# Carrying x, a 65-wide state and a 32-wide memory through the end of a four-layer scan network instead of the 512-wide rows

## What is computed

```
# four layers, 64 wide: norm, silu, complex exponential filter along the sequence,
# residual; norm, 64-256-64 network with silu, residual
h   = layers(LN(x) @ Win.T + bin)
x1  = x + LN(norm(h) @ Wout.T + bout)          # 512 wide
xn  = LN(x1)
q   = xn @ Wq.T                                # 64 wide
top = the 8 best of 128 slots by (q Wr.T)(keys Wr.T).T / sqrt(48) + log_rel
w   = softmax over these 8 of q keys.T / 8 + log_rel
mem = (w @ values) @ Wvd.T @ Wvu.T             # 512 -> 32 -> 512
g   = gate(var(xn), gelu(xn @ Wu1.T + bu1) @ Wu2.T + bu2)   # one number per row
out = x1 + LN(xn + g * mem)
```

## Time and profile before

| | us |
|---|---|
| median of three runs | 251.32 |
| the profiled execution's own time | 250.35 |
| its span in the trace | 248.5 |
| busy in the span: TensorE, VectorE, ScalarE, GpSimd | 196.7, 181.2, 128.3, 89.4 |

### The profile page before, as it was taken

How to read it: one execution, slowest core, us unless ns; L and a number is a source line. 1 busy time by engine, 2 the same in 40 slices (tenths; PEclk the granted TensorE clock), 3 DMA queues, 4 the chain that set the end, 5 groups by cost and what they waited for, 6 DMA issues and landing times.

```text
span 248.5 us, 3501 instructions
## 1 busy us (share of the span) xinstructions
PE 196.7 (79%) x1148; PEld 145.2 (58%) x1148; DVE 181.2 (73%) x507; ACT 128.3 (52%) x306; POOL 89.4 (36%) x118
## 2 busy tenths in 40 slices
PE   2699596389959998878888759999999999399600
PEld 2699495377848787767776525565556555143200
DVE  7799895557784777767663174977797775889993
ACT  4328728246543667575565644343243329587640
POOL 8213333433342443533334332121212110048772
PEclk9999989799997999999999999999999999979965
DMA  5999900000000000000000000000000000003346
GB/s 197 425 415 419 258 9 4 0 0 1 3 0 0 3 0 0 4 0 0 3 0 3 0 0 1 1 3 0 0 0 0 0 3 1 0 0 120 135 169 253
DMA packets 5407, 15.09 MB, mean 61 GB/s; under 512 B 909, under 2 KB 1773, under 8 KB 4366
## 3 DMA queue, kind: packets, MB, share of 16 engines
q1 hardware_dynamic: 5390, 14.88, 16.2%
HBM read 10.68 MB, written 4.19 MB: 60 GB/s over the span
## 4 chain that ended last, share of the span: by engine, by line
PE 49%; DVE 25%; POOL 10%; ACT 9%; issue 4%; POOLq 0%; DVEq 0%; ACTq 0%
PE bank L1164 15%; PE bank L1110 12%; POOL RS L328 8%; PE bank L1140 5%; PE bank L1057 4%; DVE Z L735 3%; DVE SS L729 3%; PE bank L1207 3%; PE bank L1070 2%; ACT SQ L449 2%; PE bank L1151 2%; DVE XT L966 2%; DVE X L972 2%; PE bank L1038 2%; PE bank L1095 1%
## 5 line engine op out<-in xcount | busy, mean ns | idle before, releaser
L328 POOL TENSOR_TENSOR RS<-SS,nhalf 128x4 f32<-128x4 f32 x36 | 43.1, 1209 | 72.0 <-DVE SS L729 71.8
L1164 PE MATMUL bank<-SW_,Y 128*128 128x384 f32 x128 | 43.9, 485 | 0.0
L729 DVE TENSOR_REDUCE SS<-SQ 128x4 f32<-128x260 f32 x36 | 15.1, 423 | 26.1 <-ACT SQ L449 25.0
L1164 PEld LDWEIGHTS bank<-SW_,Y 128*128 128x128 f32 x128 | 23.9, 190 | 17.0 <-issue 4.2
L1110 PE MATMUL bank<-ffst,HD 128*128 128x128 f32 x256 | 33.5, 287 | 0.0
L1110 PEld LDWEIGHTS bank<-ffst,HD 128*128 128x128 f32 x256 | 32.4, 205 | 0.3
L449 ACT ACTIVATE SQ<-bank 128x256 f32<-128x256 f32 x36 | 13.8, 383 | 29.4 <-PE bank L1110 18.1
L476 ACT ACTIVATE HD<-bank,b1r 128x512 f32<-128x512 f32 x32 | 20.3, 684 | 12.1 <-PE bank L1095 12.1
L1057 PE MATMUL bank<-ident,Z 128*128 128x128 f32 x64 | 11.5, 306 | 18.0 <-DVE Z L735 17.9
L1057 PEld LDWEIGHTS bank<-ident,Z 128*128 128x128 f32 x64 | 7.3, 151 | 23.7 <-DVE Z L735 23.7
L809 DVE SCALAR_TENSOR_TENSOR X<-bank,OR,X 128x512 f32<-128x512 f32 x16 | 11.3, 746 | 12.3 <-POOL OR L346 12.2
(11 more groups left out here) (219 smaller groups left out, 376.1 us busy)
## 6 DMA issues: line engine op xcount, KB each, us to landing
XT<-in_xT SPq DMA_DIRECT2D x4, 1024.0 KB, 11.4
X<-in_x SPq DMA_DIRECT2D x4, 1024.0 KB, 14.1
out<-X SPq DMA_DIRECT2D x8, 512.0 KB, 2.8
w1r<-in_w1d SPq DMA_DIRECT2D x1, 516.0 KB, 11.6
lt<-in_late SPq DMA_DIRECT2D x1, 385.5 KB, 19.3
w2r<-in_w2n SPq DMA_DIRECT2D x1, 256.0 KB, 7.1
...
```

The costliest lines, as they stand in the source:

```text
L328: pool.tensor_tensor(RS[:, g, :], SS[:, g, :], nhalf[:, :], ALU.pow).then_inc(done, 1)
L729: dve.tensor_reduce(SS[:, g, :], SQ[:, g, :, :], AX.X, ALU.add).then_inc(done, 1)
L1164: last = pe.matmul(SBK[t % 4][:, 0:SW], XNT[:, t % 4, c * P:(c + 1) * P], SW_[:, c, :], start=False, stop=(c == VC - 1))
```

## The change

The end no longer makes the 512-wide rows before it needs them. The weights of the memory's queries, of the gate and of the memory's way back are stacked beside the folded output matrix (65 columns: 64 and the bias) into M, 289 columns, centred by its column means (`column_sums`, `centre_m`). x times M is taken per tile (`project_x`, four matmuls of 289 columns into the one bank LB, and a copy, `x_out`): tiles 0 to 4 in steps 1 to 3, tiles 5 to 15 in steps 16 to 19. Norms of the 512-wide rows come out of Gram products in 65 dimensions (`gram`, `cross`, `first_variance`). `mixed` and `project` add the state's part to x's part; scores are matmuls over 64 dimensions. The memory product is 64 columns wide (`memory`), its norm comes from `dots` (32 wide), GpSimd works out the factors of a batch of tiles, VectorE writes them into the 128-wide F, which is transposed and multiplied by FM (512 columns), and `finish` adds x. All 20 steps stand before the end; `keep_busy` is gone, first_h(3) stands in step 0, and GpSimd does no 512-wide product. The score rows are 256 wide instead of 384. There are five late stages instead of six.

```diff
+ZD = DIM + 1
+MA, MQ, MU = ZD + UH + BOT, ZD + UH, ZD
+MW = ZD + UH + BOT + VB
+AW = MW - ZD
+SW = 2 * NSLOT
...
-        EARLY = 2
-        LATE0, LATES = 4, 6
-        POOL_TILES = (1, 4, 7, 10)
-        LAG = 2
+        LATE0, LATES = 4, 5
+        LATE_OUTS = (2, 4, 5, 7, 8)
+        XSTEP = {1: (0, 1), 2: (2, 3), 3: (4,), 16: (5,), 17: (6, 7, 8),
+                 18: (9, 10, 11), 19: (12, 13, 14, 15)}
+        SELS = PAIRS
+        BATCHES = ((0, 4), (4, 8), (8, 12), (12, 14), (14, 16))
+        LAST = [e // 2 - 1 for _, e in BATCHES]
+        MIXLAG = 3
+        FIN = {4: (0,), 5: (1,), 6: (2,), 7: (3,), 8: (4,), 9: (5, 6), 10: (7,)}
...
                 if g == 0:
+                    sp.dma_start(c6[:, :], c64).then_inc(s_c64, 16)
+                    sp.dma_start(WOR[:, :], woutb).then_inc(s_m, 16)
                     sp.dma_start(w2r[:, :], w2n).then_inc(s_w2, 16)
+                    sp.dma_start(M[:, :, ZD:MW], mraw).then_inc(s_m, 16)
                 if g == 1:
...
+                if s == 0:
+                    centre_m(2)
+                    centre_m(3)
...
+            centre_m(0)
+            centre_m(1)
+            for s in range(STEPS):
...
+            for a, b in BATCHES:
+                gs, w, zr, rr, al, fo, yg = (GX[:, i, a:b] for i in range(7))
+                pool.wait_ge(dots_done, b // 2)
+                pool.wait_ge(es_inv, b // 2)
+                link(pool.tensor_tensor(gs, RES[:, a:b], GA[:, 4, a:b], ALU.mult))
+                link(pool.tensor_tensor(w, gs, XQ[:, a:b, 1], ALU.mult))
+                link(pool.tensor_tensor(w, w, XQ[:, a:b, 0], ALU.add))
+                link(pool.tensor_tensor(w, w, gs, ALU.mult))
+                link(pool.tensor_tensor(w, w, K2P[:, a:b], ALU.add))
+                link(pool.tensor_tensor(zr, w, nhalf[:, 0:b - a], ALU.pow))
+                pool.tensor_tensor(yg, zr, gs, ALU.mult)
+                link(pool.tensor_tensor(rr, zr, R16[:, a:b], ALU.mult))
+                pool.tensor_tensor(F[:, a:b, ZD], rr, NXM[:, a:b], ALU.mult)
+                link(pool.tensor_scalar(al, rr, 1.0, 1.0, ALU.mult, ALU.add))
+                pool.tensor_tensor(fo, al, RHO[:, a:b], ALU.mult).then_inc(mix_ready, 1)
...
+            def mix_rows():
+                act.wait_ge(bp_mm, 1)
+                act.activation(M[:, :, 0:ZD], LB[:, 0:VC * ZD].rearrange("p (c d) -> p c d", c=VC),
+                               ACT.Copy).then_inc(bp_read, 1)
+            def column_means():
+                act.wait_ge(cs_mm, 1)
+                act.activation(CSUM[:, :], LB[:, 0:MW], ACT.Copy, scale=-1.0 / VOCAB).then_inc(cs_read, 1)
+            def x_out(t):
+                act.wait_ge(xa_mm, t + 1)
+                act.activation(XA[:, t, :], LB[:, 0:MW], ACT.Copy).then_inc(xa_read, 1)
...
+                for t in XSTEP.get(s, ()):
+                    x_out(t)
...
+            for s in range(STEPS):
+                if s == 0:
+                    mix_rows()
+                    column_means()
+                step(s)
+                if s == 0:
+                    ffn_out()
+            for p in range(PAIRS):
+                scaled(2 * p)
+                scaled(2 * p + 1)
+                gelu(p)
+                if p >= 1:
+                    qt_out(p - 1)
+            qt_out(PAIRS - 1)
+            act.wait_ge(ln_in, 1)
+            act.activation(GA[:, 3, :], GA[:, 2, :], ACT.Ln).then_inc(ln_out, 1)
+            for k in range(SELS + MIXLAG):
+                if k < SELS:
+                    exps(k)
                     e_out(k)
...
+                    y_out(k)
+                if k == 1:
+                    act.wait_ge(sig_in, 1)
+                    act.activation(GA[:, 9, :], GA[:, 8, :], ACT.Exp, scale=-1.0).then_inc(sig_out, 1)
+                if k == 2:
+                    act.wait_ge(gate_in, 1)
+                    act.activation(GA[:, 16, :], GA[:, 15, :], ACT.Exp, scale=-1.0).then_inc(gate_out, 1)
+                for p in FIN.get(k, ()):
+                    f_out(p)
...
+            def project(p):
+                for t in (2 * p, 2 * p + 1):
+                    dve.wait_ge(am_mm, 2 * p + 2)
+                    dve.wait_ge(rho_done, t // GT + 1)
+                    dve.scalar_tensor_tensor(out=T[:, t, 0:AW], in0=AB[t // GT][:, t % 2, 0:AW], scalar=RHO[:, t:t + 1],
+                                             in1=XA[:, t, ZD:MW], op0=ALU.mult, op1=ALU.add).then_inc(t_done, 1)
...
+            first_variance(2)
+            gram(3)
+            unscore(0)
+            project(2)
+            unscore(1)
+            project(3)
+            unscore(2)
+            project(4)
+            unscore(3)
+            first_variance(3)
+            project(5)
+            unscore(4)
+            gate_variance()
+            project(6)
+            unscore(5)
+            project(7)
+            unscore(6)
+            unscore(7)
+            for k in range(SELS + MIXLAG):
+                if k < SELS:
+                    select(k)
+                for i in range(len(BATCHES)):
+                    if LAST[i] + MIXLAG == k:
+                        factors(i)
+                if k == 0:
+                    for p in range(5):
+                        learned(p)
+                if k == 1:
+                    for p in range(5, PAIRS):
+                        learned(p)
+                    gate_learned()
                     gate_sum()
...
+                if k == 2:
                     gate_mean()
...
+                    gate_level()
+                if 0 <= k - 1 < SELS:
+                    dots(k - 1)
+                if k == 2:
+                    gate()
+                for p in FIN.get(k, ()):
+                    finish(2 * p)
+                    finish(2 * p + 1)
...
+            def project_x(t, s):
+                pe.wait_ge(m_done, VC)
+                pe.wait_ge(cs_read, 1)
+                if t >= 1:
+                    pe.wait_ge(xa_read, t)
+                if s > LATE0:
+                    pe.wait_ge(late_read, LATE_OUTS[LATES - 1])
+                g, j = t // GT, t % GT
+                for c in range(VC):
+                    last = pe.matmul(LB[:, 0:MW], XT[:, g, c, j * P:(j + 1) * P], M[:, c, :], start=(c == 0),
+                                     stop=(c == VC - 1))
+                last.then_inc(xa_mm, 1)
...
-            def keep_busy(n):
-                for _ in range(n):
-                    pe.matmul(T2B[:, HW:HW + P], ones[:, :], ones[:, :], start=True, stop=True)
             def turn1(u):
                 g = u % GROUPS
-                if u < 3:
-                    keep_busy(10 if u == 0 else 6)
...
-                if s + 2 < GROUPS:
-                    first_h(s + 2)
+                if s == 0:
+                    first_h(2)
+                    first_h(3)
...
+            mix_columns()
             setup_ffn()
+            column_sums()
...
+            for k in range(SELS + MIXLAG):
+                if k < SELS:
                     turn_e(k)
-                if k >= 1:
-                    memory(2 * k - 2)
-                    memory(2 * k - 1)
+                    memory(k)
+                    if k + 2 < SELS:
+                        scores(k + 2)
+                if k == 1:
+                    mean_sum()
+                for p in FIN.get(k, ()):
+                    turn_f(p, min(k + 1, SELS))
+                    output(2 * p)
+                    output(2 * p + 1)
```

More of the change, by code:

```diff
@@ L924, in first @@
[L924 to L938 removed]
+                gstep(dve.reciprocal(GA[:, 19, :], GA[:, 0, :]))
@@ new lines, in factors, with finish @@
+            def factors(i):
+                a, b = BATCHES[i]
+                dve.wait_ge(mix_ready, i + 1)
+                dve.tensor_tensor(F[:, a:b, 0:ZD], F[:, a:b, 0:ZD], rows(GX[:, 5, a:b], b - a, ZD), ALU.mult)
+                dve.tensor_tensor(F[:, a:b, 96:P], AY[:, a:b, VB:2 * VB], rows(GX[:, 6, a:b], b - a, VB),
+                                  ALU.mult).then_inc(f_done, 1)
+            def finish(t):
+                dve.wait_ge(o_mm, t + 1)
+                dve.scalar_tensor_tensor(out=X[:, t, :], in0=X[:, t, :], scalar=GX[:, 4, t:t + 1], in1=OB[t % 2][:, :],
+                                         op0=ALU.mult, op1=ALU.add).then_inc(out_ready, 1)
@@ L1004, in setup_ffn, with mix_columns, column_sums @@
                 last.then_inc(w2_mm, 1)
+            def mix_columns():
+                pe.wait_ge(s_m, 32)
+                pe.wait_ge(lt_ready, 3)
+                for c in range(VC):
+                    last = pe.matmul(LB[:, c * ZD:(c + 1) * ZD], WOR[:, c * P:(c + 1) * P], LT[:, :], start=True,
+                                     stop=True)
+                last.then_inc(bp_mm, 1)
+            def column_sums():
+                pe.wait_ge(bp_read, 1)
+                for c in range(VC):
+                    last = pe.matmul(LB[:, 0:MW], ones[:, :], M[:, c, :], start=(c == 0), stop=(c == VC - 1))
+                last.then_inc(cs_mm, 1)
@@ L1029, in setup_late @@
```

(56 more changed lines are left out.)

678 lines of the change are left out of this document (326 added, 352 removed).

## The result

| | before | after |
|---|---|---|
| median of the runs of this comparison, us | 251.45 (4 runs) | 288.65 (4 runs, 286.57 to 290.42) |
| the profiled execution, us | 250.35 | 286.57 |
| its span, us | 248.5 | 284.8 |
| busy: TensorE, VectorE, ScalarE, GpSimd, us | 196.7, 181.2, 128.3, 89.4 | 215.6, 156.5, 113.1, 82.7 |

After to before is 1.1476, interval 1.1376 to 1.1576: 14.8% slower. The forecast was 260.9 us with a range up to 269. The direction was right, the size was not, and no rival came near it. VectorE did lose 25 us of work, and the program still became 36 us longer.

A forecast was written before the change was run, and what follows sets the result against it. No single engine was taken to bound the program: a latency loop in the middle, then a matmul-bound stage, then nothing full. Span 248.5 + 8.7 - 2.1 - 19.5 + 18.5 + 4 = 258.1, with 2.8 added 260.9 us; range 247 to 269.

The forecast's parts named there:

- Part 1: Steps 0 to 3: x tiles, column_sums and copies of x ahead of ScalarE's squares delay turn1(4), +8.7 us.
- Rival (c): Steps 1 and 2: copies of x do not hold the squares, +3 instead of +8.7, 255 us; chance 0.18.
- Part 2: Steps 4 to 15, without x: narrower score rows and a filled TensorE gap outweigh a longer late stage, -2.1 us.
- Part 3: Steps 16 to 19 and the projection up to scores: 56.6 us at full clock instead of 76.1, -19.5 us.
- Part 4: Last loop: from iteration 4 finishes wait for their own iteration's whole way through in-order TensorE; 64.0 instead of 45.5, +18.5 us.
- Part 5: Clock: TensorE's pauses in the last loop bring the 1.2 GHz level, 1.0 us in each of iterations 4 to 7, +4.
- Rival (b): The slow clock holds through the whole end, +10 instead of +4 us, 267 us; chance 0.22.
- Rival (a): Last loop, iterations 4 to 7: bound by VectorE's own work, 18.2 instead of 31.0 us, total 244 us; chance 0.22.

The follow-up runs named there:

- e1: Changed kernel with matmuls of ones, results unused, in TensorE's pauses from the last gram to the end: span 267.9 us against 284.8, ratio to before 1.075.
- e7: Changed kernel with ScalarE's squares of steps 2 and 3 ahead of its copies of x of the step before: span 277.5 us against 284.8.
- e9: Changed kernel with a second PSUM bank for every other tile of x in steps 18 and 19: span 286.1 us against 284.8.
- e2: Changed kernel with turn_f and output ahead of turn_e, and f_out ahead of the exponentials, in the last loop: span 264.5 us against 284.8, median time 269.21.
- e11: Changed kernel with turn_f and output first, x tiles 5 to 11 in steps 9 to 15, squares ahead of x copies, no fills: 247.09 us, ratio to before 0.9862.
- e5: Changed kernel with turn_f and output first, matmuls of ones in TensorE's pauses, x tiles 5 to 11 in steps 9 to 15: 245.15 us, ratio to before 0.9774.

## Why the prediction was wrong

The forecast of the time was 27.75 us too low. 26.7 of it are in the span; the rest is that the forecast added 2.8 us to the span, and the median is 3.85 over that of the profiled execution. The stages of the walk beside what was measured, in us of span:

| stage | predicted | measured | miss |
|---|---|---|---|
| to turn1(4) | 63.45 | 64.18 | +0.7 |
| turn1(4) to turn1(16) | 70.1 | 70.2 | +0.1 |
| to the last gram | 41.3 | 46.0 | +4.7 |
| to select(0), at full clock (e1) | 15.3 | 18.2 | +2.9 |
| last loop, at full clock (e1) | 64.0 | 70.0 | +6.0 |
| the clock in both (22.1 - 18.2, 82.4 - 70.0) | 4.0 | 16.3 | +12.3 |
| sum | 258.1 | 284.8 | +26.7 |

**Part 1 was right, by its mechanism and its size.** The start is late by +9.4, +8.7 were forecast, and e7 shows the cause: with the squares ahead of the copies turn1(4) comes within 1.8 us of before, part of it through the clock that stays up. Rival (c), that the copies would not hold the squares, is out. The Trainium skill's rule on SBUF's two separate sides ("SBUF — State Buffer") would have made it +10.4. The traces agree that these instructions hold each other up. GpSimd's pair centre_m(0) and (1), then one of VectorE's table products with two SBUF inputs in the changed kernel, and the same product before:

```profile
18.23 1.74 POOL L372 TENSOR_TENSOR M<-M,CSUM 128x289 f32<-128x289 f32 x2 [3.96 <-ACT CSUM L488]
19.23 1.02 DVE L740 TENSOR_TENSOR tmpB<-cvst,CS 128x256 f32<-128x256 f32 x1
...
19.93 0.42 DVE L656 TENSOR_TENSOR tmpB<-cvst,CS 128x256 f32<-128x256 f32 x1
```

A second one, beside centre_m(3), took 1.16 instead of 0.68 us: 1.1 us together. How much of it reaches turn1(4), no run separates, so the 0.7 us between forecast and measurement stay unassigned.

**Part 2 was right:** 70.2 us, and the clock was 1.00 in it.

**Part 3 was mis-sized.** The gap between tiles was put at 0.66 us; the tiles follow every 2.89 instead of 2.60, and e9 shows that the bank is the reason, as the text said. Seven such tiles make 2.0 of the 4.7. Most of the rest is step 18, 13.1 us where 10.75 were forecast, at whose end TensorE waits 1.23 us for the last state. Before select(0), 1.6 of the 2.9 are a wait that the sum doesn't have. It gave 1.5 us to gram(3)'s product and sum, but in VectorE's order a projection of two tiles, which waits for `mixed` behind the last gram on TensorE, and first_variance(2) stand ahead of them. In e1, where the last gram ends at 179.73:

```profile
180.58 0.81 DVE L929 SCALAR_TENSOR_TENSOR XT<-bank,RHO,XA 128x224 f32<-128x224 f32 x2 [11.58 <-PE bank L1316]
...
182.23 0.69 DVE L908 TENSOR_REDUCE OC<-V 128x8 f32<-128x520 f32 x1
```

The next instruction starts at 182.84, 3.1 us behind the gram. From there to the last projection's end it took 12.0 instead of 10.9 us. The gate's rows (`unscore`) are 0.6 of that: a pair of them takes 0.52 us and not 0.42.

**Part 4 had the right mechanism** (the finishes hang on their own select, by TensorE's order), which e2 confirms: with the order changed the loop falls by 20.65 us in the profiled execution, the clock's return in its second half included, and e11's, with the same order, lasts 62.1. Its sizes were low, but for iterations 0 to 3 (17.5 us in e1, 18.7 forecast). In e1, at full clock, select to finish took 232.48 - 227.08 = 5.4, not 4.75; memory is 0.66, not 0.3. And the last finishes were miscounted: iteration 9 finishes two pairs, so four pairs follow iteration 7, not three. They took 15.0 us instead of 11.1.

**Part 5 is the step that failed.** "I take 1.0 for each of iterations 4 to 7, since such slow stretches lasted only 3 to 4 us" was worked out from gaps of before that stood alone between dense stretches. Here the clock stays at 0.50 from 202 to 234 us, and from there to 265 us its mean is 0.67. Even that mean hides something: the clock came back behind the output pair, when TensorE had nothing to do, and was low again for the next iteration's matmuls (windows of iteration 5, the pause and the memory product with the first scores):

```profile
234.00:237.50 3.50, 0.00 (x0) 0.00 (x0) 3.00 (x13) 0.89 (x4) 0.00 (x0) 0.93 0.40 150
238.40:240.00 1.60, 1.56 (x8) 1.15 (x8) 0.00 (x0) 0.23 (x1) 0.00 (x0) 0.50 0.00 0
```

The price of one iteration is the difference of the two shown, the changed kernel's and e1's, 7.8 - 5.4 = 2.4 us to the first finish; I had bounded it at 2 and taken 1. From select to select, iterations 4 to 6 took 13.8, 11.4 and 10.1 us against 9.8, 8.8 and 7.8 in e1, that is 4.0, 2.7 and 2.3; another 2.5 stand behind the start of select(7), 1.0 in iterations 0 to 3, and 3.9 before select(0), to which the forecast gave nothing. Rival (b), the slow clock through the whole end, was the case that came, and even it was priced at +10 where 16.3 were paid. With that term alone right, the sum of spans would have been 270.4; the other 14.4 us are sizes, nearly all in parts 3 and 4.

**Rival (a)** asked for VectorE as the bound. It is never full in the loop. That e5's time, 245.15, is near the rival's 244 is chance: e5 also moves x, which is worth 14.6 us alone, and its loop of 58.6 us, VectorE busy 39.3 of it, is not the 51.2 (64.0 - 12.8) of the rival.

**Where the expected gain went.** Stage by stage against the kernel before: +9.4 to turn1(4), -1.9 to turn1(16), 68.0 instead of 76.1 to select(0), which is -8.1 where -19.5 was forecast, and +36.9 in the loop; together +36.3. A stage that was bound by matmuls, with TensorE full at the high clock, became in large part a latency loop with pauses. The old loop had VectorE busy 35.87 of its 45.50 us; the new one has it busy 39.27 of 82.40.
